# A perceiver stack on one Trainium2 core: the query stage and the cross attention of each layer as one program

## What is computed

```
x = x + L0_xattn(layernorm(x), ctx)      # 32 query heads, 8 key heads, keys = context and the 32 latents
x = x + L0_attn(layernorm(x))            # a Taylor mixture and a gated feed forward ("Mixer")
x = x + L0_ffn(layernorm(x))             # gated feed forward with low-rank parts ("Lora")
x = x + L1_xattn(layernorm(x), ctx, mask)# as the first, keys = context only, with a mask
x = x + L1_attn(layernorm(x))            # causal self attention with rotary positions
x = x + L1_ffn(layernorm(x))             # 16 experts, top 2, and a shared one
```

```
q = rms_norm((x @ Wq) per head, q_w)     # 256 tokens x 32 heads x 128
k = rms_norm((kv @ Wk) per head, k_w)    # 8 heads
v = (kv @ Wv) per head
out = softmax(q k^T / sqrt(128)) v       # 4 query heads share a key head
x += out @ Wo
```

## Time and profile before

| | |
|---|---|
| runs shown | 1554.22, 1553.94, 1551.43 us, median 1553.94 us |
| the profiled execution | 1552.46 us, of which span 1550.7 us |
| mean granted clock of TensorE | 0.983 of full speed |
| PE | 1499.5 us busy, 97% |
| DVE | 891.7 us, 58% |
| ACT | 731.1 us, 47% |
| POOL | 313.4 us, 20% |
| HBM traffic | 99.36 MB moved by DMA, 64 GB/s over the span |

### The profile page before, as it was taken

The page is one execution under the profiler, slowest core; times in us unless marked ns, Lnnn a source line. Parts: engine busy times, 40 slices in busy tenths (PEclk is TensorE's granted clock), DMA queues, the critical chain, the costliest instruction groups (busy, mean ns, idle before and its releaser), DMA issues. The chain is left out here.

```text
span 1550.7 us, 23628 instructions
## 1 busy us (share of the span) xinstructions
PE 1499.5 (97%) x8240; PEld 1273.8 (82%) x8240; DVE 891.7 (58%) x1702; ACT 731.1 (47%) x1359; POOL 313.4 (20%) x498
## 2 busy tenths in 40 slices
PE   8999999999999999979898999999999999998898
PEld 6878888888888888868677888888888888886787
DVE  6735555555545555748576555555555555676565
ACT  5634454544544445637255444344444444563443
POOL 2322222222222121023233222221122222000000
PEclk9999999999999999989999999999999999999899
DMA  8110000000000003357071000000000001241242
GB/s 326 43 65 28 18 26 19 19 25 15 34 17 21 25 13 114 109 183 240 3 279 48 21 8 28 7 20 20 7 27 14 14 20 61 82 177 48 82 162 95
DMA packets 29162, 99.36 MB, mean 64 GB/s; under 512 B 7024, under 2 KB 7536, under 8 KB 23504
## 3 DMA queue, kind: packets, MB, share of 16 engines
q1 hardware_dynamic: 29104, 98.60, 18.0%
HBM read 95.83 MB, written 2.75 MB: 64 GB/s over the span
## 5 line engine op out<-in xcount | busy, mean ns | idle before, releaser
L54 PE MATMUL c0a_kbanks<-c_wkv_lo_r,c_cT_hi 128*128 128x512 f32 x320 | 132.0, 412 | 4.0 <-PEq L455 3.0
L54 PE MATMUL c1a_kbanks<-c_wkv_lo_r,c_cT_hi 128*128 128x512 f32 x320 | 132.0, 412 | 2.4 <-PEq L455 1.2
L56 PE MATMUL c0a_kbanks<-c_wkv_hi,c_cT_lo_r 128*128 128x512 f32 x320 | 126.2, 394 | 0.0
L56 PE MATMUL c1a_kbanks<-c_wkv_hi,c_cT_lo_r 128*128 128x512 f32 x320 | 125.7, 393 | 0.0
L55 PE MATMUL c1a_kbanks<-c_wkv_hi,c_cT_hi 128*128 128x512 f32 x320 | 125.7, 393 | 0.0
L55 PE MATMUL c0a_kbanks<-c_wkv_hi,c_cT_hi 128*128 128x512 f32 x320 | 125.4, 392 | 0.0
L1526 ACT ACTIVATE c1a_p<-c1a_sm,c1a_nmax 128x512 f32<-128x512 f32 x64 | 46.4, 725 | 132.7 <-DVE c1a_nmax L1618 132.7
L1600 DVE TENSOR_TENSOR g_stage_r<-c0a_ktbank,c0a_kT_hi 128x512 fp32r<-128x512 f32 x64 | 44.3, 692 | 110.4 <-ACT c0a_kT_hi L1515 110.4
L1526 ACT ACTIVATE c0a_p<-c0a_sbank,c0a_nmax 128x544 f32<-128x544 f32 x64 | 45.9, 717 | 125.5 <-DVE c0a_nmax L1611 125.5
L1547 ACT ACTIVATE c1a_sq<-c1a_kbanks 128x512 f32<-128x512 f32 x64 | 38.3, 598 | 141.2 <-PE c1a_kbanks L56 141.2
L54 PE MATMUL c0a_vbank<-c_wkv_lo_r,c_cT_hi 128*128 128x512 f32 x256 | 100.6, 393 | 0.0
(11 more groups left out here) (484 smaller groups left out, 4220.6 us busy)
## 6 DMA issues: line engine op xcount, KB each, us to landing
c_cT_lo<-in_ctx SPq DMA_DIRECT2D x64, 256.0 KB, 2.5
c_wkv_lo<-in_l_wo SPq DMA_DIRECT2D x16, 1024.0 KB, 4.7
g_stage<-in_l_wq SPq DMA_DIRECT2D x15, 1024.0 KB, 5.0
e_stage<-in_e_w SPq DMA_DIRECT2D x20, 768.0 KB, 4.2
c_wkv_lo<-in_l_wkv SPq DMA_DIRECT2D x8, 1024.0 KB, 7.0
m_stage<-in_mix_ffn SPq DMA_DIRECT2D x10, 768.0 KB, 5.4
c_vlat<-vlat_dram SPq DMA_DIRECT2D x32, 64.0 KB, 1.8
m_tw_lo<-in_mix_out SPq DMA_DIRECT2D x1, 1792.0 KB, 12.1
```

Source lines behind the costliest of these rows:

```text
L54: nc.tensor.matmul(out, a[0], b[1], start=start, stop=False)
L56: return nc.tensor.matmul(out, a[1], b[0], start=False, stop=stop)
```

## The change

The two functions no longer open blocks. Each returns a set of five programs, and `cross_attention` runs the query stage's program and then the attention's on each engine in one block, with no meeting of the engines between them. For c1, the transposes of rounds 14 and 15 and their placing go to the first step of the attention. The attention's PSUM is ordered so that its key banks are the two that the query stage does not use (c0) or has used only for the Mixer and the Lora block (c1), and its value bank is pbank0. SBUF tiles are reordered so that tiles of the attention's first step do not lie on those that the query stage still needs.

```diff
+        with nc.Block() as block:
+            attends = []
+            @block.gpsimd
+            def _(pool):
+                asked.gpsimd(pool)
+                early.close()
+                attends.append(attend(nc, ctx, tag + "a", g, w, kvw, qT, q_place, mask, klatT, vlat, context, wo,
+                                      vl_stored, const, const_set, border, follow))
+                attends[0].gpsimd(pool)
+            @block.sync
+            def _(sp):
+                asked.sync(sp)
+                attends[0].sync(sp)
...
+class Border:
+    def __init__(self, placed, cleared, turn, place):
+        self.placed, self.cleared, self.turn, self.place = placed, cleared, turn, place
```

In `queries` (the constants for POOL now come from outside, one set for both stages; NL is 0 in c1):

```diff
+    CLEAR_AT = 4
...
-                    if ahead and n == N0 - 1:
+            if ahead and n == CLEAR_AT:
                 pool.wait_ge(kvw.loaded[0], 16)
                 sm.retire()
                 sf.retire()
...
-                for n in range(NN - LAG, NN):
-                    transposes(n)
+        transposes(pe, NN - LAG)
...
-                    for n in range(NN - LAG, NN):
-                        place(n)
+            place(act, NN - LAG)
...
+    def turn_late(pe, i):
+        if NL:
+            if i == 0:
+                pe.wait_ge(vl_rest, 1)
+        else:
+            transposes(pe, NN - LAG + 1 + i)
+    def place_late(act, i):
+        if not NL:
+            place(act, NN - LAG + 1 + i)
+    return (Programs(sync, gpsimd, tensor, scalar, vector),
+            Border((placed, NN), (rstd_ready, CLEAR_AT + 1), turn_late, place_late))
```

In `attend`:

```diff
-        kbanks = s.ps("kbanks", 2)
-        kbank = [kbanks[:, i * 512:(i + 1) * 512] for i in range(2)]
-        vbank = s.ps("vbank")
-        ktbank = s.ps("ktbank")
-        sbank = s.ps("sbank", 2)
-        pobanks = s.ps("pobanks", 2)
+    sbank = s.ps("sbank", 2)
+    vbank = s.ps("vbank")
+    ktbank = s.ps("ktbank")
+    pobanks = s.ps("pobanks", 2)
+    kbanks = s.ps("kbanks", 2)
...
+    def sync(sp):
+        sp.wait_ge(*border.cleared)
...
+    def gpsimd(pool):
+        def step(b, hf):
+            opening = is_at(b, 0) and hf == 0
+            at = 2 if opening else 0
...
+                if k == at:
+                    if opening:
+                        pool.wait_ge(*border.placed)
                     need(pool, s_done, UNIT_H * (u - 1))
                     nc.gpsimd.tensor_copy(flat(q[0]), mine).then_inc(q_hi, 1)
```

POOL's wait for `vl_stored` (c0 only) goes from its start to the lo half of the latents' keys in unit 0 (`latent_keys`), and DVE's to step 1. TensorE, then ScalarE, then VectorE:

```diff
+            opening = is_at(b, 0) and hf == 0
...
                 project(k, hf, kbank[k % 2]).then_inc(k_proj, 1)
+                if opening and k == 0:
+                    border.turn(pe, 0)
...
                 project(k, 2 + hf, vbank).then_inc(v_proj, 1)
+                if opening and k == 0:
+                    border.turn(pe, 1)
```

```diff
                 elif k > 0:
                     place_k(n - 1, hf, k - 1, u)
+                else:
+                    border.place(act, 0)
...
                 nc.scalar.activation(v[:, hf, k, :], vbank[:], ACT.Copy).then_inc(v_ready, 1)
+                if not attends and k == 0:
+                    border.place(act, 1)
```

```diff
                 elif k > 0:
+                    if tail and k == 1:
+                        dve.wait_ge(vl_stored, 32)
                     lo_of_k(n - 1, hf, k - 1)
...
-                if tail:
-                    dve.wait_ge(vl_stored, 32)
```

More of the change, by code:

```diff
@@ new lines, in transposes, with place @@
+    def transposes(pe, n):
+        if n < 0:
+            return
+        k = n % SLOTS
+        pe.wait_ge(normed, n + 1)
+        need(pe, placed, n - 1)
+        for h in range(UNIT_H):
+            last = nc.tensor.transpose(tbank[k % 2][:, h * P:(h + 1) * P],
+                                       xn[:, k, h * P:(h + 1) * P], ident[:])
+        last.then_inc(transposed, 1)
+    def place(act, n):
+        if n < 0:
+            return
+        bank = tbank[n % 2][:, :]
+        act.wait_ge(transposed, n + 1)
+        if n < N0:
+            tile, t = divmod(n, TT)
+            nc.scalar.activation(
+                qT[:, t * BT:(t + 1) * BT, tile * UNIT_H:(tile + 1) * UNIT_H, :],
+                bank.rearrange("p (h b q) -> p b h q", h=UNIT_H, b=BT),
+                ACT.Copy, scale=nk[:, 3:4]).then_inc(placed, 1)
+        else:
+            half, t = divmod(n - N0, TT)
+            nc.scalar.activation(klatT[:, half * UNIT_H:(half + 1) * UNIT_H, t * P:(t + 1) * P],
+                                 bank.rearrange("p (h k) -> p h k", h=UNIT_H),
+                                 ACT.Copy).then_inc(placed, 1)
@@ L1169, in add, with attend @@
                                      ALU.add).then_inc(self.added, 1)
-def attend(nc, tag, g, w, eps, kvw, qT, q_place, mask, klatT, vlat, context, wo, vl_stored, follow):
+def attend(nc, ctx, tag, g, w, kvw, qT, q_place, mask, klatT, vlat, context, wo, vl_stored, const, const_set, border,
+           follow):
     ident = g["ident"]
@@ new lines, in attend @@
+    ot_ready = s.sem("ot_ready")
+    LAST = UNIT_H * (UNITS - 1)
+    out = OutputProjection(nc, s, g["x"], qT, wo, context, kbank, ot_ready, v_proj)
+    PARTS = len(out.PARTS)
+    after = None
+    if follow is not None:
+        spare = Region(nc, "s", nc.sbuf_base, SBUF_END)
+        after = SelfAttention(nc, s, g, follow, spare,
+                              Region(nc, "s", start, nc.sbuf_base), Region(nc, "s", kvw.start, kvw.end),
+                              {"first": (vbank, ktbank), "second": kbank, "wide": (sbank, pobanks)})
+        moe = Experts(nc, Space(nc, ctx, "e"), g, follow, Region(nc, "e", spare.at, SBUF_END),
+                      Region(nc, "e", *q_place), Region(nc, "e", context.start, context.end),
+                      Region(nc, "e", start, nc.sbuf_base), Region(nc, "e", kvw.start, kvw.end),
+                      {"turn": [sbank[:, i * 512:(i + 1) * 512] for i in range(2)], "router": ktbank,
+                       "gate": [pobanks[:, i * 512:(i + 1) * 512] for i in range(2)],
+                       "y": [after.ybank(t) for t in range(TT)]})
@@ new lines, in attend, with last_unit, unit_before, run @@
+    WO_LAST_UNIT = ((), (0,), (1,), (2, 3))
+    WO_FINISH = ((4, 5), (6, 7), (8, 9, 10), (11,))
+    def last_unit(b, hf):
+        return is_at(b, B - 1) and hf == 1
+    def unit_before(j):
+        return (B - 1, 1, j - 1) if j else (B - 1, 0, UNIT_H - 1)
+    def run(eng, slot_step, finish):
+        def both(b):
+            slot_step(b, 0)
+            slot_step(b, 1)
+        peeled(eng, B, both)
+        finish()
+    def sides(bank):
+        return bank[:, :].rearrange("p (a n) -> p a n", a=2)[:, :, 0:HALF]
@@ L1735 @@
+    return Programs(sync, gpsimd, tensor, scalar, vector)
 class GatedTiles:
```

1530 lines of the change are left out of this document (734 added, 796 removed).

## The result

The changed kernel takes 1539.94 us (median of four executions, 1536.92 to 1541.4) against 1552.91 us (four, 1551.43 to 1554.22) for the kernel before: a ratio of 0.9914, interval 0.9896 to 0.9933, or 13.0 us less. The forecast was 1540.9. The profiled execution took 1536.92 us, of which the span is 1535.1. It is the fastest of its four, so its trace shows a little more gain than the medians do.

A forecast was written before the change was run, and what follows sets the result against it. TensorE, busy 97% of the span, bounds the kernel; gains of 4.82 (c0) and 7.53 us (c1) at the borders sum to 12.35, from a middle of 1553.2 to 1540.9. Range 1538.5 to 1542.5, to 1546 with two rivals.

The forecast's parts named there:

- c0's border: From the query stage's last matmul to step 1's key projection in c0: gain 4.82 us, 3.11 idle, 1.69 clock, 0.02 value projection.
- The spare time of `kn`: In c0's first attention step, `kn` ends at 95.4, ahead of key transposes at 97.04, with 1.6 us to spare.
- VectorE's new wait for the stored values: In c0's step 1, DVE waits for the store of the values; claimed 2 us to spare, so no delay.
- c1's border: Up to step 1's key projection in c1: gain 7.53 us, 6.30 waits and meeting plus 2.19 clock, less 0.96 moved transposes.
- The spare times: In c1's first attention step, inputs of rounds 14 and 15 and `kn` end before TensorE asks, so projections hide the waits.
- Rival (b): Round 14's or 15's chain comes late on DVE or ACT; TensorE waits 3.27 us inside step 0: 1544.2 us, chance 5%.
- The split into waits and clock: At both borders, part of the gain is regained clock, 1.69 us in c0 and 2.19 in c1, the rest mainly waits.
- Freeing the semaphores: POOL's freeing moves from c1's round 15, where it cost 1 us, to round 4, where its price is nothing.
- SP: SP reaches its new wait at 811.9, after round 4, so it does not stop; its small loads land in time.
- The layout: The new order of banks and tiles changes no instruction's shape: costed at nothing, bounds 0.5 us either way.
- The loop's returns: Turns of the batch loop, 12 in both layers: moved code could make them cost more or less; a return costs up to 0.56 us.
- rival (c): Moved code makes each of 12 loop turns dearer, 28.7 us more in all: 1569.6 us, chance 4%.

## Why the prediction came out right, step by step

**c0's border: right.** The forecast was 4.82 us by the two starts, and the table has 4.82. The first key matmul follows the last one of the query stage by 0.23 us without a wait. Step 1's key projection was forecast at 94.31 from a start of 88.62; the trace has 94.79 from 89.11, or 5.68 against 5.69. The spare time of `kn` was 1.77 us, forecast as 1.6. VectorE's new wait for the stored values made nothing late: TensorE has no idle time in step 1.

**c1's border: right, 7.74 against 7.53.** The transposes of rounds 14 and 15 cost less than the 0.48 a set that I took: keys to values to keys is 832.54 - 826.16 = 6.38 us, against 2 x 3.21 = 6.42, and the two rounds ahead take 0.79 (826.16 - 825.37), against 0.96. The old border took 15.61 us in two traces, 14.97 and 14.61 in two others, so this fit is closer than the old border repeats. The waits of the earlier trace rows are gone. The spare times held: round 14's `xn`, the row at 826.81 below, ends at 827.49 and is asked for at 829.00, 1.5 us later where I had 1.6. Round 15's ends at 829.29 and is asked for at 832.19, 2.9 us later where I had 2.0. `kn` of step 0 ends at 832.67 and is asked for at 835.38. Rival (b) didn't happen.

```profile
826.81 0.68 DVE L723 TENSOR_TENSOR c1q_xn<-c1q_pbank,c1q_rstd 128x512 f32<-128x512 f32 x1
```

**The split into waits and clock: right in kind.** Two blocks bring the clock's price back, one program without the late transposes does not. Its size in c1 varies with the old border.

**Freeing the semaphores: right.** In round 4 POOL loses 3.33 us on issue, more than the 2.51 it was idle for before, and no matmul waits:

```profile
793.32 0.20 POOL L563 TENSOR_TENSOR c1q_ms<-c1q_ss,c_const 128x4 f32<-128x4 f32 x1 [3.33 <-issue]
```

The same edit in round 15 of one program wasn't tried, because the attention's own semaphores then take the freed numbers before they are cleared.

**SP: right.** It comes to the mask behind the query weights, at 806.08, and TensorE waits for none of the small tables.

```profile
798.18 7.85 SPq L153 DMA_DIRECT2D g_stage<-in_l_wq  x2
...
806.08 1.84 SPq L1334 DMA_DIRECT2D c_mask<-in_mask  x4
```

**The layout: wrong.** This is the step of the sum that failed: "The new order of banks and tiles changes no instruction's shape. I cost it at nothing; its bounds are 0.5 us either way". The order of banks does cost nothing. The addresses of the SBUF tiles cost 0.053 us in the median step of c1 and 2.74 us in all. Beside it the query stages became 0.23 and 0.45 us shorter, in all kernels with the changed kernel's layout alike (63.16 to 63.20 and 37.27 to 37.31, before 63.40 and 37.74), and c0's attention 0.37. The net of the layout is therefore about 2.74 - 1.05 = +1.7 us, more than three times the bound. "No instruction changes its shape" was no reason for a bound: an address isn't a shape, and this edit is one that shifts every later tile.

**The loop's returns: wrong in sign.** Rival (c) reckoned with dearer turns. In c1 the turns cost 0.36, 0.51, 0.25, 0.24, 0.24, 0.24 and 0.08 us over a plain step with two blocks, and 0.14 and four times 0.12 with one program; c0's attention shows none in either. That is about 1.3 us less at the turns; over c1's whole attention one program takes 1.05 us less than two blocks with the changed tiles (492.02 against 493.07) and 1.09 less with the old addresses (489.24 against 490.33). It appears in every kernel with one program and in none with two, so the place of the code goes with it; that the place is the cause is argued, not shown. It is what the Trainium skill's "Runtime: NRT & Kernel Launch", section "Instruction fetch mechanics", leaves possible: a branch out of the pages that an engine holds has to fetch its target. The trace agrees with it in so far as the price of a turn changed (0.36 and 0.51 us became 0 and 0.14 at the first two) while the loop's own code stayed the same. No run here shows the fetch.

Together: 12.58 at the borders and 1.05 in c1's attention by the one program, less 1.7 for the layout, are the table's 11.9 us. The medians of the three sessions differ by 13.0, 11.8 and 11.6 us. That the sum of 12.35 fitted so well is partly luck, because the two errors point in opposite directions.

**What beats both.** The changed kernel with the old addresses took 1534.96 us where the changed one took 1537.33 in the same session, 2.4 us less, and its trace has 2.78 less in the very part that was asked about. The two intervals overlap, though each of the four executions is shorter than each of the six; the step of 7.920 against 7.973 us, in the one profile of each, is what carries it.

**What stays open.** Which other access meets the matmuls at the positions of the table isn't settled: the delayed ones move when the tiles move, in ways that neither the bank order nor a multiple of 64 bytes explains. The delayed matmuls read weights and context tiles that did not move, so it is another tile's place that counts; I didn't try moving one tile at a time.

## What to carry to other kernels

A meeting of the engines between two stages costs the wait of the bound engine, and it can cost a slow restart as well, 1.7 to 2.2 us at the borders here, so price both, and check with the timeline whether what the meeting waited for is needed at all. Moving a tail of dependent small work behind the next stage's first independent piece was worth 2.77 us on top of the one program at c1's border; with the meeting kept, the border had only 2.64 of the 7.76 us, the earlier freeing of the semaphores included. After any edit that inserts or removes a tile ahead of others, compare the length of one steady step in both traces, as 50 ns in a step of 8 us add up to nearly 3 us over 60 steps and nothing on the page points at them.

## What the runs showed of the hardware

A shift of the attention's SBUF tiles from `kT_hi` to `rstd` by 32 bytes lengthened the distance behind some matmuls of 512 columns in c1 by 4 to 9 ns (from 227 to as much as 236), at fixed positions of the step, and the step from 7.920 to 7.973 us; 64 bytes gave 7.980 with other positions. The new order of PSUM banks gave 7.920. In c0 the same shift of all tiles left the attention as it was (507.50 us against 507.46), so an address alone doesn't set the price; what beside it does isn't shown.

At the borders, TensorE's granted clock stayed at full speed (2.4 GHz) after 1.4 us and after two times 1.1 us of idle time. Stretches at the lower level (1.2 GHz), with means of 0.50 to 0.57 over the windows read, followed idle times of 2.95 us and of 8.1 us, and the waits of 1.13, 2.14 and 1.18 us at c1's old border. The same wait of 2.71 us elsewhere had one in 10 of 13 traces. A low clock during the idle time costs nothing: 8.1 us of idle time cost 11.14, and the 3.0 beyond the wait are half of the 5.8 us of low clock in the work behind it.

In parts whose code was the same in all kernels the clock was low for 17.1 to 23.9 us in the rest of layer 0 and for 6.8 to 20.5 in the rest of layer 1, from one trace to the next, and the latter took 205.37 us at the one end and 210.9 at the other. A single trace of this kernel can't tell 3 us in those parts from nothing. The borders of the changed kernel repeat to 0.01 us in its three traces; c1's old border went from 14.61 to 15.61.
